# One query tile in eight takes its row maximum by pairs of keys, and TensorE sends its score tiles out one by one

## What is computed

```python
q, k, v = split(x @ w_qkv)                       # (4, 16, 1024, 8) each
attn = einsum('bhid,bhjd->bhij', q, k) * scale + phi_bias(L)
attn = softmax(attn, axis=-1)                    # over 1024 keys
out  = einsum('bhij,bhjd->bhid', attn, v) @ w_proj + b_proj
```

## Time and profile before

| | us |
|---|---|
| median of 3 runs | 1120.49 |
| lowest, highest | 1118.1, 1120.71 |
| the profiled execution | 1122.93 |
| its span, first to last instruction | 1121.1 |

### The profile page before, as it was taken

One profiled execution on the slowest core, in us unless ns is written; L12 is line 12 of the kernel. 1 busy time (PEld: TensorE's weight loads), 2 busy tenths in 40 slices (PEclk: granted clock), 3 DMA queues, 4 the chain that ended last, 5 costly groups with the idle time before them and its releaser, 6 DMA issues. The chain is left out here.

```text
span 1121.1 us, 36169 instructions
## 1 busy us (share of the span) xinstructions
PE 980.0 (87%) x11663; PEld 548.3 (49%) x11667; DVE 911.8 (81%) x1801; ACT 726.9 (65%) x1573; POOL 358.1 (32%) x468
## 2 busy tenths in 40 slices
PE   5529998574999999999999999999999998639996
PEld 4429998340333333333333333333333346639996
DVE  6447886547999999999999999999999976548885
ACT  1114443470888888888888888888888884224443
POOL 1623444003232323232332323232333323524343
PEclk9999999695899999999999999999999997569998
DMA  9612221686122222222222222222222444622220
GB/s 305 239 63 67 67 66 35 171 278 171 51 72 72 69 69 60 75 73 60 74 64 71 72 64 69 69 69 69 61 76 71 103 106 171 236 71 71 63 67 26
DMA packets 84957, 106.70 MB, mean 95 GB/s; under 512 B 15835, under 2 KB 68065, under 8 KB 84368
## 3 DMA queue, kind: packets, MB, share of 16 engines
q1 hardware_dynamic: 79344, 93.51, 28.7%
q0 software_dynamic: 5568, 12.63, 3.2%
HBM read 74.14 MB, written 36.55 MB: 99 GB/s over the span
## 5 line engine op out<-in xcount | busy, mean ns | idle before, releaser
L1126 DVE TENSOR_REDUCE nmax<-psS 128x1 f32<-128x1024 f32 x512 | 600.7, 1217 | 39.1 <-PE psS L979 31.5
L1269 ACT ACTIVATE big<-psE 128x512 f32<-128x512 f32 x1024 | 553.0, 598 | 101.5 <-PE psE L964 98.9
L964 PE MATMUL psE<-qop,kop 122*32 122x512 bf16 x4096 | 319.0, 386 | 4.5 <-ACT big L1269 3.0
L1341 POOL TENSOR_TENSOR big<-big,const 128x512 f32<-128x512 f32 x128 | 162.7, 1271 | 443.2 <-ACT big L1269 443.2
L997 PE MATMUL psV<-big,vst 128*9 128x256 f32 x4096 | 265.9, 379 | 1.3
L979 PE MATMUL psS<-maxop 32*128 32x512 bf16 x1024 | 176.7, 395 | 28.3 <-DVE nmax L1126 13.3
L997 PEld LDWEIGHTS psV<-big,vst 128*9 128x9 f32 x4096 | 101.4, 90 | 115.7 <-issue 12.4
L964 PEld LDWEIGHTS psE<-qop,kop 122*32 122x32 bf16 x4096 | 90.7, 96 | 132.0 <-ACT big L1269 59.7
L979 PEld LDWEIGHTS psS<-maxop 32*128 32x128 bf16 x1024 | 48.0, 91 | 188.7 <-issue 114.6
L733 ACT ACTIVATE siga<-psGa,w1sa 128x128 f32<-128x128 f32 x156 | 44.6, 368 | 61.0 <-PE psGa L645 61.0
L733 ACT ACTIVATE sigb<-psGb,w1sb 128x128 f32<-128x128 f32 x156 | 44.6, 368 | 60.7 <-PE psGb L645 60.7
(11 more groups left out here) (190 smaller groups left out, 924.9 us busy)
## 6 DMA issues: line engine op xcount, KB each, us to landing
maxop<-qk_parts SPq DMA_DIRECT2D x256, 64.0 KB, 1.9
qop<-qk_parts SPq DMA_DIRECT2D x64, 144.0 KB
kop<-qk_parts SPq DMA_DIRECT2D x64, 144.0 KB
weighted_sums<-osum SPq DMA_DIRECT2D x64, 128.0 KB
qk_parts<-part SPq DMA_DIRECT2D x16, 384.0 KB, 3.6
xsa<-sorted_a SPq DMA_DIRECT2D x39, 128.5 KB, 2.1
xsb<-sorted_b SPq DMA_DIRECT2D x39, 128.5 KB
w1a<-in_w SPq DMA_DIRECT2D x1, 4128.0 KB
```

Source lines behind the costliest of these rows:

```text
L964: last = nc.tensor.matmul(psE[BANK[turn]][32 * c:32 * c + 32, :], kop[b][0:TROWS, lo:lo + 32], qop[b][0:TROWS, half * HALF:(half + 1) * HALF],
L1126: nc.vector.tensor_reduce(nmax[r % 2][:, qt:qt + 1], psS[n % 2][:], AX.XY, ALU.max, negate=True).then_inc(s_max, 1)
L1269: nc.scalar.activation(prob[r % 2][:, lo:lo + HALF], psE[BANK[16 * (r % NBUF) + n]][:], ACT.Exp).then_inc(s_exp, 1)
L1341: nc.gpsimd.tensor_tensor(dst, dst, diag[:, 4 * h:4 * h + 4, :], ALU.mult).then_inc(s_diag, 1)
```

## The change

Four things change in `phase_attention_last`.

1. TensorE's order: for p from 0 to 3 it is now score(2p), weigh(2p), gather(2p), score(2p + 1), weigh(2p + 1), gather(2p + 1), where gather takes one key tile. Each score tile stands alone between a gather and a weigh.
2. Score tile 3 (`PAIRED`) is computed in another way. GpSimd negates the queries of that tile in the band of the second key half (`turn_round`). The second matmul then has 64 rows of operands, both bands, so that it gives score(key j) - score(key j + 512). ScalarE takes Relu of its negative into `more` (128 by 512), and VectorE adds the first half's scores to `more` and takes the maximum of the sums in one instruction over 512 elements (`tensor_tensor_reduce`), in place of its reduction over 1024.
3. The maxima are no longer negated; the last two rows of `kbias` are -1 instead.
4. ScalarE's copy of the sums comes before the first exponential of the step, and its Relu before the seventh.

```diff
-        nmax = [m.sb(f"nmax{s}", [P, KT]) for s in range(2)]
+        qmax = [m.sb(f"qmax{s}", [P, KT]) for s in range(2)]
+        more, junk = m.sb("more", [P, HALF]), m.sb("junk", [P, HALF])
+        PAIRED = [3]
...
                     if n == 0:
-                        pe.wait_ge(s_mop[b], 64 * filled(q, r, 2))
+                        pe.wait_ge(s_less, i + 3)
...
                     for half in range(2):
-                        lo = 32 * (u + half)
+                        both = half == 1 and n in PAIRED
+                        lo, hi = 32 * (u + half - both), 32 * (u + half) + SROWS
                         last = nc.tensor.matmul(psS[n % 2][:, half, :],
-                                                maxop[b][lo:lo + SROWS, 0, qt % 4 * P:(qt % 4 + 1) * P],
-                                                maxop[b][lo:lo + SROWS, 1, :], start=True, stop=True)
+                                                maxop[b][lo:hi, 0, qt % 4 * P:(qt % 4 + 1) * P],
+                                                maxop[b][lo:hi, 1, :], start=True, stop=True)
...
                 for p in range(4):
+                    if live(at, 2):
+                        score(2 * p)
                     if live(at, 0):
                         weigh(2 * p)
+                    if live(at, -1):
+                        gather(2 * p)
                     if live(at, 2):
-                        score(2 * p)
                         score(2 * p + 1)
                     if live(at, 0):
                         weigh(2 * p + 1)
                     if live(at, -1):
-                        gather(p)
+                        gather(2 * p + 1)
...
+                        if n in PAIRED:
+                            dve.wait_ge(s_more, len(PAIRED) * (i + 2) + PAIRED.index(n) + 1)
+                            dve.sem_inc(s_go, 1)
+                            nc.vector.tensor_tensor_reduce(
+                                out=junk[:], in0=psS[n % 2][:, 0, :], in1=more[:], scale=1.0,
+                                scalar=-3.0e38, op0=ALU.add, op1=ALU.max,
+                                accum_out=qmax[r % 2][:, qt:qt + 1]).then_inc(s_max, 1)
...
+                    if live(at, 2) and n % 4 == 2 and n // 2 in PAIRED:
+                        k = PAIRED.index(n // 2)
+                        act.wait_ge(s_s, 8 * (i + 2) + n // 2 + 1)
+                        if k == 0 and later(at, 2, 1):
+                            act.wait_ge(s_max, 8 * (i + 1) + PAIRED[-1] + 1)
...
+                        nc.scalar.activation(more[:], psS[n // 2 % 2][:, 1, :], ACT.Relu, scale=-1.0)\
+                            .then_inc(s_more, 1)
...
+            def turn_round(b, age):
+                pool.drain()
+                pool.wait_ge(s_mop[b], 64 * age)
+                for n in PAIRED:
+                    lo, c = 32 * (2 * (n % 2) + 1), ORDER[n] % 4 * P
+                    tile = maxop[b][lo:lo + SROWS, 0, c:c + P]
+                    nc.gpsimd.tensor_tensor(tile, none[lo:lo + SROWS, 0:1].to_broadcast([SROWS, P]), tile,
+                                            ALU.subtract)
+                    pool.drain()
+                pool.sem_inc(s_less, 1)
+
+            pool.drain()
+            for b in range(2):
+                turn_round(b, 1)
...
                     for h in range(2):
+                        if h == 1 and live(at, 3):
+                            turn_round((r + 3) % NBUF, filled(q, r, 3))
...
-    kbias[6 * KT:] = np.ones((2, L), bf16)
+    kbias[6 * KT:] = -np.ones((2, L), bf16)
```

## The result

The changed kernel takes 1175.55 us (median; 1174.23 to 1176.29) against 1119.81 for the kernel before: 1.0498 times, 95% interval 1.048 to 1.0517. It is 5% slower. The profiled execution took 1175.33 us, with a span of 1173.3.

> The changed kernel once more, to be read beside the others on the same chip: 1174 to 1179.

The account below looks back on a forecast made before the run. Bound before: TensorE and VectorE in a closed loop, 10.01 us a step; after, TensorE. Halves 10.36, paired tile 0.32, copy 0.17, loop's turn 0.10 make 10.95: +51.2 over steps 1 to 61, +3.2 at the start; median 1175, range 1150 to 1193.

Parts of the forecast that it names:

- The price that had no row: TensorE's change from gather to score, absent before the change: bounds 0.215 and 0.32 us, taken as 0.32.
- rival A: Score weights load while gather runs, so that change is free: step 9.91 + 0.10, 1117 to 1121 us; chance 0.08.
- The half: TensorE's score, weigh, gather sequence for one score tile, half of a p: 1.295 us, eight a step making 10.36.
- The closed loop of the kernel before: TensorE's scores and VectorE's reductions wait for each other: 5.00 us for two stretches, 10.0 a step.
- The paired tile: Tile 3's second matmul on TensorE can't run beside its first: 0.32 us a step, bounds 0.215 and 0.32.
- The copy: ScalarE's copy delays gather 0.35 us every second step, 0.17 a step (bounds 0 and 0.35), with 0.05 for the semaphore.
- One sign of mine: In the changed trace, VectorE and ScalarE idle before every tile, ended by TensorE; VectorE under 90% busy.
- The loop's turn: Where the hardware loop turns, once in four steps: 0.10 us a step kept, taking 10.85 to 10.95.
- The start: Before full steps: first score's wait for GpSimd 0.9 us, two score-only steps +0.5, step 0 +1.8; 3.2 in all.
- B: Rival: the 0.10 come of the closed loop, not the shape, and vanish with it: step 9.2, 1070 us; chance 0.09.
- C: Rival: ScalarE's Relu keeps weigh's buffers longer, 0.2 to 0.6 us a step: 1190 to 1210; chance 0.11, table load included.
- (D): Rival: VectorE's paired instruction takes no less than 1.13 us, changing nothing while TensorE is the bound; no chance given.

Follow-up runs that it names:

- e4: Changed kernel without pairing, score weights zero-padded to the 128-row by 32-column shape of weigh and gather: 1261.1 us, ratio 1.1255.
- e11: Changed kernel without pairing, only score tiles 1 and 5 zero-padded to the shape of weigh and gather: 1155.4 us, ratio 1.0307.
- e1: Changed kernel without pairing; single score tiles and the early copy stay, all tiles reduced over 1024 scores: 1156.82 us, ratio 1.0322.
- e5: Kernel before with each VectorE reduction over the first 512 keys only, TensorE's work and order unchanged: 1051.98 us, ratio 0.9391.
- e2: Changed kernel with TensorE's order and the copy's place as before, so pairing of tile 3 alone: 1139.17 us, ratio 1.0169.
- e12: e2 with score tile 5 paired as well as tile 3: 1129.52 us, ratio 1.0087.
- e7: Changed kernel with the copy of the sums put back behind the step's first exponential: 1202.96 us, ratio 1.0732.
- e3: Changed kernel with the first gather of a step moved behind weigh(1): 1173.73 us, ratio 1.0474.
- e10: Changed kernel without pairing, each half of a score tile sent out alone, sixteen score stretches a step instead of eight: 1982.2 us, ratio 1.7677.

## Why the prediction was right

**The price that had no row.** Gather to score, 0.32 or 0.215: 0.32 in the changed kernel, 0.43 for two groups when the shapes are equal (e4, e11). That decided between my case and rival A. The half was worked out as 1.295 and is 1.30; e1's step is 8 halves and the wait for the copy.

**The closed loop of the kernel before.** e5 and e2 bear it out, and e12, which goes the way that two chains ask for. Not right in it was TensorE's own time in pairs: the second tile starts with the first and not 0.09 after it, which makes 8.76 of the 9.0 that I gave for e5. It changes nothing in the sum, only what the old order was worth.

**The paired tile.** 0.32 on TensorE: 0.31 to its second weights, and e1 is 0.32 a step (10.99 - 10.67) faster. In time, 19 to 21 us. Relu 0.60 (0.58 predicted), the addition 0.69 and 0.08 more for the accumulator, `turn_round` 0.40: all hidden, as costed. VectorE's step is 9.2 (544.46 / 59) and not 8.9, which the cover takes too. One sign of mine didn't show: VectorE has no idle time before every tile, but waits for Relu and then works off five.

**The copy, mis-sized.** The sum had 0.35 in two steps; it is 0.54. The step that failed is "with 0.05 for the semaphore": gather starts 0.26 (after) and 0.22 (e7) after the copy's end. The copy itself runs when it was said to. For a score that waits for VectorE, and for a weigh that waits for ScalarE (27 times in e3 and e5), the next weights do start 0.05 after the end of what they waited for; gather(0) has four waits in a row, and the instructions of TensorE's queue for them stand before the first weights. I showed the distance, and the weigh rules out that ScalarE's signal as such is the slower one; that the further waits fill the rest was not tested.

A row of the kernel before already had this price. The prediction says that there the copy hides; it does in only every second odd step, and in the others gather waits 0.26 for it and starts 0.23 after its end (533.37), though the closed loop takes the wait up and the step stays at 10.02:

```profile
532.79 0.58 ACT L1277 COPY osum<-psV 128x512 f32<-128x512 f32 x1
...
532.90 0.62 PE L964 MATMUL psE<-qop,kop 122*32 122x512 bf16 x8
...
533.60 1.05 PE L997 MATMUL psV<-big,vst 128*9 128x256 f32 x16
```

**The loop's turn, mis-sized the other way.** I kept 0.10 a step. A turn of the changed kernel is 43.97 us; four steps of 8 x 1.30 + 0.32 and two waits of 0.54 are 43.96. So next to nothing of the 0.37 a turn is left, and the traces tell why: most of it was no cost of the loop. In the kernel before the steps of a turn take 10.01, 10.30, 10.10 and 10.01, and the 0.29 is a wait of the turn's last group of weigh:

```profile
520.16 0.90 PE L964 MATMUL psE<-qop,kop 122*32 122x512 bf16 x8
520.66 0.10 PEld L964 LDWEIGHTS psE<-qop,kop 122*32 122x32 bf16 x4 [0.40 <-ACT big L1269]
```

Three buffers don't divide the 64 groups of a turn, so `BANK` (line 849) gives the last group buffer 1, which was used two groups earlier and not three; its exponential is not done, and two groups take 0.90 instead of 0.61. That weigh starts 1.07 after the one before it (519.09). In the changed kernel they are 1.30 apart, ScalarE is nearly done, and the last group starts 0.29 after its neighbour instead of 0.23: 0.06 a turn are left. In e5, where they are 0.86 apart, the wait is 0.49, and in e12 it is 0.49 as well. The step of 10.10 is the one behind that wait; how it comes by its 0.09 isn't shown, and no run changed the list of buffers.

The two errors, the copy's and the turn's, are +0.10 and -0.10 a step and cancel, 6 us each; the step came out as 10.99 against 10.95.

**The start.** It came out as worked out. The first score starts 1.0 us after GpSimd's first instruction (0.9), from it to the first score of step 0 it is 18.75 us against 18.24 (0.5), and step 0 takes 12.64 against 10.82 (1.8).

**What was luck.** The median lies within 1 us of the prediction, while the terms were right to about 6 us. Between the two profiled executions the span grew by 52.2 us: 60 steps +53.1, the start +3.3, everything from the first score of step 61 on -0.9, and -3.3 in the part ahead of the attention, which the change doesn't touch (GpSimd's first instruction of the phase at 257.02 instead of 260.33; 258.26 in the repeated run).

**Rivals.** A and B fell with the first half in the trace: no change of shape is free. C, ScalarE keeping weigh's buffers, doesn't show in the changed kernel beyond the 0.06 a turn, but e3 shows that it lies close: as soon as four weigh groups stand near each other, a buffer is late. No table is loaded for Relu: one load stands among the exponentials, as before, and none at Relu's line. (D) fell with the 0.69 and 0.08 against 1.13.

## What to carry to other kernels

Read what a change of the matmul's shape costs from the distances of the starts, not from busy time, and count the changes before an order is refined: here an alternation takes the waits away, but it doubles the number of changes, and they cost more than the waits did. Where two engines wait for each other in turn, neither one's idle time is slack: work out the loop, see whether it is several interleaved chains, and put a saving and its price into the same chain. A wait that is lifted from one place (the copy) comes back in part as a wait for the next resource in line (a buffer), so cost a move with all queues that it passes. And where every fourth step is longer, look for the wait in that step before calling it the price of the loop: here it was a buffer that came round one group too early.

## What the runs showed of the hardware

- Where weights of 32 rows by 128 columns follow weights of 122 or 128 rows by 32 columns, or the other way round, the starts are 0.32 us apart instead of 0.22, and 0.54 instead of 0.44 at 1.2 GHz; 64 rows after 32 are 0.31 apart.
- Four matmuls of 32 rows in four bands run at once (0.40 for four in e5, 0.39 for one pair); the price of single tiles is as much this (four times 0.215 a step) as the change of shape (eight times 0.10).
- A loop body with 48 matmuls more a step fetches its instructions again in each turn (145 packets against 23). TensorE pauses there for 3 to 4 us and in most turns once more for about 2, and the granted clock is 0.5 for some 7 us behind the first pause; with 12 more a step there is none of this.
- With halves of tiles sent out alone TensorE, busy throughout, stays at 1.2 GHz until the last of them, and reads 2.4 GHz soon after, when it does only weigh and gather (e10).
- Weights that wait for one semaphore start 0.05 us after the end of the awaited instruction; those of gather(0), with four waits ahead of them, 0.22 to 0.25 us after it.
- `tensor_tensor_reduce` runs as two instructions, 0.69 and 0.08 us for 512 elements, and the next reduction starts right with the second (505.11 both).
